# Edge rounds of a fused graph kernel: tile sums in two banks in turn, weights' sums made anew in each round, the third gather ahead of the edge rows, node products' parts made ahead of the rounds

## The reference, cut to what matters

```python
h = x @ W
agg = jnp.einsum('ben,bnf->bef', alpha, h)                      
beta = jax.nn.sigmoid((h @ a_gn)[:, None, :] + (agg @ a_ge)[:, :, None])
all_he = jax.nn.elu(beta[..., None] * h[:, None, :, :] + (1.0 - beta[..., None]) * agg[:, :, None, :])
logits2 = jnp.where(H[None, :, :] > 0, se[:, None, :], NEG)
coefs1 = jax.nn.softmax(logits2, axis=-1)
g = jnp.einsum('bne,benf->bnf', coefs1, all_he)
```

## Time and profile before

| | |
|---|---|
| median of 3 runs | 725.89 us (724.87 to 726.29) |
| the profiled execution's own time | 726.31 us |
| its span in the profile | 724.1 us |
| PE busy | 668.4 us, 92% of the span |
| DVE, ACT, POOL busy | 422.0, 340.6, 289.9 us |
| mean granted TensorE clock | 0.97 |
| the eight edge rounds | 102.8 to 195.8 us |

### The profile page before, as it was taken

One profiled execution on the slowest core, in us unless ns is written; L12 is line 12 of the kernel. 1 busy time (PEld: TensorE's weight loads), 2 busy tenths in 40 slices (PEclk: granted clock), 3 DMA queues, 4 the chain that ended last, 5 costly groups with the idle time before them and its releaser, 6 DMA issues.

```text
span 724.1 us, 9828 instructions
## 1 busy us (share of the span) xinstructions
PE 668.4 (92%) x3420; PEld 462.6 (64%) x3428; DVE 422.0 (58%) x966; ACT 340.6 (47%) x655; POOL 289.9 (40%) x267
## 2 busy tenths in 40 slices
PE   6898989788799989999999999999999999999993
PEld 2796766566566867633333348887777777778883
DVE  1675656767539852366878756314565767651166
ACT  0861234544366651265666643323446556455214
POOL 0270104565536720010324256122667676760045
PEclk9999999999989699999999999999999999999998
DMA  9120030000000027000100000000000000000013
GB/s 326 38 88 2 1 116 1 1 0 1 1 2 1 4 52 164 19 0 1 37 22 1 1 0 1 1 1 1 2 1 1 0 1 1 1 1 2 1 29 87
DMA packets 14995, 18.34 MB, mean 25 GB/s; under 512 B 10128, under 2 KB 10128, under 8 KB 14944
## 3 DMA queue, kind: packets, MB, share of 16 engines
q1 hardware_dynamic: 14432, 16.06, 7.7%
q10 hardware_dynamic: 512, 1.60, 0.6%
HBM read 11.37 MB, written 2.10 MB: 19 GB/s over the span
## 4 chain that ended last, share of the span: by engine, by line
PE 53%; POOL 8%; DVE 6%; ACT 4%; issue 2%; ACTq 0%; POOLq 0%; DVEq 0%
PE PS L1504 9%; PE PS L1391 7%; PE PS L1374 7%; PE PS L1517 5%; POOL LN_Y L163 4%; PE PS L1557 4%; PE PS L1546 4%; PE PS L182 2%; PE PS L1483 2%; PE PS L1490 2%; PE PS L189 2%; PE PS L1567 2%; DVE arena L2143 2%; DVE LN_ST L140 1%; PE PS L1420 1%
## 5 line engine op out<-in xcount | busy, mean ns | idle before, releaser
L2143 DVE SCALAR_TENSOR_TENSOR arena<-PS,WT,arena 128x256 f32<-128x256 f32 x160 | 77.5, 484 | 49.2 <-PE PS L1517 27.0
L1714 ACT ACTIVATE arena<-PS,spare 128x1024 f32<-128x1024 f32 x64 | 70.8, 1109 | 49.8 <-DVE spare L2080 49.6
L2080 DVE TENSOR_REDUCE spare<-PS 128x1 f32<-128x1024 f32 x64 | 75.6, 1219 | 23.8 <-PE PS L1374 23.7
L1504 PE MATMUL PS<-WH,KK 128*128 128x512 f32 x256 | 86.1, 402 | 0.1
L163 POOL TENSOR_TENSOR LN_Y<-LN_V,CN 128x16 f32<-128x16 f32 (+1 forms) x18 | 50.0, 2779 | 67.6 <-DVE LN_V L155 67.6
L1782 ACT ACTIVATE spare<-PS,WT 128x256 f32<-128x256 f32 x96 | 38.8, 471 | 63.7 <-DVE arena L2143 61.8
L1875 POOL TENSOR_TENSOR arena<-arena,spare 128x128 f32<-128x128 f32 x32 | 13.8, 433 | 134.2 <-DVE spare L2086 123.6
L1391 PE MATMUL PS<-arena 128*64 128x512 f32 x256 | 62.0, 605 | 1.5 <-POOL arena L1875 1.4
L1504 PEld LDWEIGHTS PS<-WH,KK 128*128 128x128 f32 x256 | 48.0, 187 | 16.7 <-issue 5.7
L1504 PE MATMUL PS<-WL,KK 128*128 128x512 f32 x128 | 50.0, 391 | 0.0
L1374 PE MATMUL PS<-arena 64*128 64x512 f32 x192 | 48.2, 617 | 1.4 <-ACT arena L1714 1.4
(11 more groups left out here) (293 smaller groups left out, 1496.8 us busy)
## 6 DMA issues: line engine op xcount, KB each, us to landing
arena<-in_adj_tr SPq DMA_DIRECT2D x8, 512.0 KB, 5.9
arena<-in_x_tr SPq DMA_DIRECT2D x4, 512.0 KB, 8.0
arena<-in_x_nat SPq DMA_DIRECT2D x1, 2048.0 KB, 9.0
arena<-arena SPq DMA_DIRECT2D x7, 256.0 KB, 2.8
arena<-arena SPq DMA_DIRECT2D x12, 128.0 KB, 2.3
spare<-in_w SPq DMA_DIRECT2D x2, 512.0 KB, 4.0
out<-arena SPq DMA_DIRECT2D x4, 256.0 KB, 3.1
out<-arena SPq DMA_DIRECT2D x8, 128.0 KB, 2.2
```

Of the source, the lines that this page charges most:

```text
L1504: ins = pe.matmul(acc, x[:, t % 2, b, :], w[:, k, c], start=(first and n == 0), stop=(not first and n == 2), skip_group_check=True)
L1714: act.activation(EF[2 * (i % RING) + par], banks("S", 2 * i + par).rearrange("p a c -> p (a c)"), ACT.Exp, bias=NMX[:, i, par:par + 1], ac ...
L2080: dve.tensor_reduce(NMX[:, i, par:par + 1], banks("S", 2 * i + par), AX.XY, ALU.max, negate=True).then_inc(max_ready, 1)
L2143: dve.scalar_tensor_tensor(acc, PS[:, four_banks(t, j), d * F:(d + 1) * F], WT[:, e:e + 1], acc, ALU.mult, ALU.add).then_inc(acc_step, 1)
```

## The change

- The sums of the tiles lie in bank 4 for even tiles and in bank 7 for odd ones, so PE zeroes a bank without waiting for the copy of the tile before (it waits for that of the tile before the last one).
- The weights' sums no longer run on over a tile: each round starts them afresh in bank 5, ACT copies them out to a new ZR (128 x 8) and POOL adds ZR into ZS, which it has zeroed at the start. POOL's addition waits for ACT's copy (`zr_out`) and stands at the end of the round, ahead of L383 and L387. PE waits for the copy of the round before (`zr_out`) ahead of the edge rows, as these write bank 5 too. DVE's reciprocal waits for the additions (`zs_added`).
- PE has gather C ahead of the edge rows. DVE has shift A ahead of the interval tests.
- All eight `high` stand on ACT behind the tanh (L484), ahead of the second industry copy; all eight `low` on POOL ahead of the register loads. PE waits for all of them ahead of the first gather.

```diff
@@ -289,7 +289,13 @@
 iota = CN[:, C_IOTA:C_IOTA + ROUND].rearrange("p (c n) -> p c n", n=P)
-SMALL_AT, ZN_AT = CHUNKS * E, 0
+SMALL_AT, ZN_AT = CHUNKS * E, 3 * P
+ZR = sb("ZR", [P, B])
+zr_out, zs_added = sem("zr_out"), sem("zs_added")
+
+def sums_bank(t):
+    return 4 + 3 * (t % 2)
+
 A_, B_, C_ = range(CHUNKS)
@@ -351,6 +357,7 @@
         pool.memset(zero16[:, :], 0.0).then_inc(zero_set, 1)
+        pool.memset(ZS[:, :, :], 0.0)
         pool.wait_ge(sl, 1)
@@ -362,8 +369,8 @@
-        low(0)
-        low(1)
+        for t in range(NT):
+            low(t)
         first = first_rounds(pool)
@@ -376,8 +383,8 @@
                                        ALU.mult).then_inc(w_ready, 1)
-            if t + 2 < NT:
-                low(t + 2)
+                pool.wait_ge(zr_out, j + 2)
+                pool.tensor_tensor(ZS[:, t, :], ZS[:, t, :], ZR[:, :], ALU.add).then_inc(zs_added, 1)
             if t >= 1:
@@ -483,14 +490,17 @@
                            bias=wt(W_FCB, 1)).then_inc(the_done, 1)
+
+        def high(t):
+            act.activation(HPH[:, t, :], HP[:, t, :], ACT.Copy).then_inc(hph_ready, 1)
+
+        for t in range(NT):
+            high(t)
         industry_out(1)
...
-        def high(t):
-            act.activation(HPH[:, t, :], HP[:, t, :], ACT.Copy).then_inc(hph_ready, 1)
-
         def edges_out(dst, done):
@@ -508,12 +518,11 @@
         act.activation(AGS[:, :], PS[:, 7, :], ACT.Copy).then_inc(agh_ready, 1)
-        high(0)
         first = first_rounds(act)
+        act.activation(ZR[:, :], zero16[:, 0:B], ACT.Copy).then_inc(zr_out, 1)
         industry_out(3)
...
         act.activation(AGM1[:, :], bits(AGS[:, :]), ACT.Copy, scale=-1.0).then_inc(agn_ready, 1)
-        high(1)
         industry_out(4)
@@ -553,11 +562,9 @@
                 likely()
-            if t + 2 < NT:
-                high(t + 2)
-            act.wait_ge(acc_done, first[t + 1] + 1)
-            act.activation(GN[:, t, :], PS[:, 4, :], ACT.Copy)
-            act.activation(ZS[:, t, :], PS[:, 7, ZN_AT:ZN_AT + B], ACT.Copy).then_inc(acc_out, 1)
+                act.wait_ge(acc_done, j + 2)
+                act.activation(ZR[:, :], PS[:, 5, ZN_AT:ZN_AT + B], ACT.Copy).then_inc(zr_out, 1)
+            act.activation(GN[:, t, :], PS[:, sums_bank(t), :], ACT.Copy).then_inc(acc_out, 1)
@@ -744,10 +751,10 @@
                 mix(A_, 2)
+                shift(A_, 2)
                 dve.wait_ge(selg_ready, j + 1)
...
                 from_first(at).then_inc(ns_half, 1)
-                shift(A_, 2)
                 dve.wait_ge(ns_half, j + 2)
@@ -765,9 +772,10 @@
             if t >= 1:
-                dve.wait_ge(acc_out, t)
+                dve.wait_ge(zs_added, first[t])
                 dve.reciprocal(ZS[:, t - 1, :], ZS[:, t - 1, :]).then_inc(rn_ready, 1)
         dve.wait_ge(acc_out, NT)
+        dve.wait_ge(zs_added, first[NT])
         dve.reciprocal(ZS[:, NT - 1, :], ZS[:, NT - 1, :]).then_inc(rn_ready, 1)
@@ -965,7 +973,7 @@
         pe.wait_ge(agn_ready, 1)
-        pe.wait_ge(hpl_ready, 1)
+        pe.wait_ge(hpl_ready, NT)
         pe.wait_ge(nsg_ready, 1)
@@ -975,22 +983,21 @@
         for t in range(NT):
-            if t >= 1:
-                pe.wait_ge(acc_out, t)
-            pe.matmul(PS[:, 4, :], zero16[:, 0:P], zero16[:, :], start=True, stop=False, skip_group_check=True)
-            pe.matmul(PS[:, 7, ZN_AT:ZN_AT + B], zero16[:, 0:P], zero16[:, 0:B], start=True, stop=False, skip_group_check=True)
-            pe.wait_ge(hpl_ready, min(t + 2, NT))
+            if t >= 2:
+                pe.wait_ge(acc_out, t - 1)
+            pe.matmul(PS[:, sums_bank(t), :], zero16[:, 0:P], zero16[:, :], start=True, stop=False, skip_group_check=True)
             with pe.Fori(first[t], first[t + 1]) as j:
...
                     pe.wait_ge(w_ready, CHUNKS * j + (c + 1))
-                    return pe.matmul(PS[:, 4, :], NST[:, c, :], S1[:, c, :], start=False, stop=True, skip_group_check=True)
-
+                    return pe.matmul(PS[:, sums_bank(t), :], NST[:, c, :], S1[:, c, :], start=False, stop=True, skip_group_check=True)
+
+                pe.wait_ge(z_ready, CHUNKS * j + 1)
+                gather(t, C_)
+                pe.wait_ge(zr_out, j + 1)
                 pe.wait_ge(ns_ready, j + 2)
                 edge_rows(t_next)
-                pe.wait_ge(z_ready, CHUNKS * j + 1)
-                gather(t, C_)
                 pe.wait_ge(nst_out, j + 1)
@@ -1007,8 +1014,8 @@
                 for c in range(CHUNKS):
-                    ins = pe.matmul(PS[:, 7, ZN_AT:ZN_AT + B], NST[:, c, :], CC[:, c, :], start=False, stop=True,
-                                    skip_group_check=True)
+                    ins = pe.matmul(PS[:, 5, ZN_AT:ZN_AT + B], NST[:, c, :], CC[:, c, :], start=(c == 0),
+                                    stop=(c == CHUNKS - 1), skip_group_check=True)
                 ins.then_inc(acc_done, 1)
```

## The result

The changed kernel took 761.96 us, the median of 4 runs (761.63 to 762.42); the kernel before took 726.05 on the same chip (724.87 to 726.29). The ratio is 1.050, 95% interval 1.048 to 1.052. The direction was forecast, the size was not: 732.1 us, with a range up to 736.8.

A forecast was written before the change was run, and what follows sets the result against it. Rounds were bound by the PE and DVE chain to the first scatter, with POOL's queue to take over. Terms 3.0 + 1.2 + 0 - 0.5 + 1.0 + 1.5 = + 6.2 gave 732.1 us; range over the cases 726.8 to 736.8.

The forecast's parts named there:

- sum of + 6.2 us: Whole kernel: 3.0 + 1.2 + 0 - 0.5 + 1.0 + 1.5 us slower, giving 732.1 us.
- rival C: Edge rounds: two opened waits bring two to three further low-clock stretches, 1.3 us each; 735 to 737 us, chance 0.16.
- The prediction's last sentence: Wrong if rounds 2 to 6 scatter before T + 4.3, or more or fewer half-clock rounds make over 3 us.
- 0 in itself: PE's gather C, moved from a covered place into the idle stretch behind T, costs nothing: 0 us.
- The wait for L623 came behind that one and ended later: 0: Two banks: PE's dropped wait for ACT's copy ahead of the zeroing was covered by a later wait: 0 us.
- POOL's queue paces rounds 2 to 7: POOL sets the first scatter at T + 4.9 (4.4 to 5.4): + 3.0 us, and + 1.2 in round 7; chance 0.61.
- Edge rows, turn, round 1: Edge rows about T + 1.5, unhindered scatter T + 3.8, turn done by T + 4; round 1 unchanged, about 10.6 us.
- Round 0: First round, POOL empty: earlier edge rows count, - 0.5 us (0 to - 1.2).
- Front: Ahead of the rounds: POOL's eight parts meet seven DVE instructions and delay L712's loop, + 1.0 us (0 to + 1.3).
- End: End of the stage: POOL still has the addition, L383 and L387 for tile 6, + 1.5 us (1.3 to 1.7).
- A: Rounds 2 to 6: POOL's steps fit before the first product is needed, DVE's relief decides; 724.2 us, chance 0.12.
- B: Whole kernel: gains and losses cancel, POOL's queue at its lower bound, one low-clock stretch less; 725.9 us, chance 0.11.

The follow-up runs named there:

- e3: The changed kernel with matmuls of zeros in both PE waits of a round, 5 behind the edge rows and 6 ahead of the first scatter: 736.78 us.
- e1: The changed kernel with POOL's addition of ZR behind the two output steps of the tile before: 740.11 us.
- e4: The changed kernel with gather C behind the edge rows again, POOL's queue left as changed: 752.3 us.
- e8: The changed kernel with POOL's addition behind the output steps and gather C behind the edge rows again: 726.28 us.
- e14: The changed kernel plus PE's old wait for ACT's copy of the tile just done, ahead of the zeroing: 745.38 us.
- e10: e1 plus PE's old wait for ACT's copy of the tile just done, ahead of the zeroing: 724.32 us.
- e2: The kernel before with POOL's two output steps of the previous tile waiting for the round's end: 729.26 us.
- e11: The changed kernel with only PE's wait behind the edge rows filled, by 5 matmuls of zeros: 739.07 us.
- e12: The changed kernel with only PE's wait ahead of the first scatter filled, by 6 matmuls of zeros: 742.74 us.
- e9: e1 plus 5 matmuls of zeros in PE's wait behind the edge rows: 721.66 us.
- e16: The kernel before plus 5 matmuls of zeros (384 columns) ahead of the edge rows' wait: 723.09 us.
- e15: e1 plus 8 matmuls of zeros once, ahead of round 0: 737.14 us.
- e17: e1 plus 13 matmuls of zeros once, ahead of round 0: 731.5 to 745.0 us, ratio 1.0126.

## Why the prediction was right in its sign and wrong in its size

**The term of the clock failed.** The sum of + 6.2 us has no term for the clock; about 25 of the 36 us are the clock. It stood in rival C alone, as "Two to three further stretches, 1.3 each". There the sign and the places were right: it named the two waits behind the edge rows and before the first scatter. The number was low, four more than before in rounds 2 to 7, and the price far too low. 1.3 was read from rounds in which the clock was down for 3.4 us (164.6 to 168.0). Now it stays down over most of the round (136.7 to 146.9). Before, the fall was followed at once by gather C; now by the wait for POOL, scatter A and the small sums. Whether that is the reason for its length is not shown. The round at 0.69 costs 16.78 - 12.37 = 4.4 us, with e3's round as the measure. From T of round 0 to T of round 7 the changed kernel took 109.43 us and e3 87.63, 21.8 less; with the 3.9 by which e3's round 0 ended earlier that is the 25. The prediction's last sentence names this as a sign of being wrong: rounds at half clock that make up more than 3 us.

**"0 in itself" for gather C** failed with it. Its time was hidden before and after, as said; what it did where it stood was not, since it was the one piece of wide work among edge rows, turn and wait. Moved, it leaves a stretch of 4 us with 1.17 us of matmuls in it. It cost 9.7 to 13.8 us (e1, e4, e8).

**"The wait for L623 came behind that one and ended later: 0"** for the two banks failed in the same way. As a wait the old one was indeed covered. But it cut PE's idle time in two, ahead of gather C and behind it, and put back it returned 16.6 us to the changed kernel and 15.8 to e1 (e14, e10).

**POOL's queue paces rounds 2 to 7:** right in four of the six, and under-sized. In one of the others DVE's comparison, itself held back beside POOL, came last, in the other it tied with the product; the turn stood at T + 4.76 and T + 4.51, not by T + 4. The first scatter came at T + 5.43 in five of the six rounds (4.94 in the other), not 4.9, at the upper end of 4.4 to 5.4. Of the sum, the addition took 0.60, L394 1.59 against 1.27, and the first of the two L384 about 1.36 (2.40 - 1.04) beside DVE's L749. All three are meetings with DVE; alone the addition took 0.20, at 231.33 below. By the Trainium skill ("SBUF — State Buffer", section "SBUF: two separate sides") a DVE instruction with two SBUF inputs and a GpSimd instruction exclude each other for a whole instruction. The trace agrees, with 5.43, and with the L749 that started 0.05 us behind an L394 of 1.26 and took 1.75 instead of 0.69. The term is 5 x 1.11 + 1.74 = 7.3 at most, instead of 4.2. On the kernel before, POOL's two steps kept behind the round's end cost 3.3 (e2).

**Edge rows, turn, round 1:** the relief of DVE was forecast at T + 1.5 for the edge rows and T + 3.8 for an unhindered scatter; measured T + 1.20, and T + 3.78 in e1. Round 1 took 10.62, as said. Rounds 2 to 7 at full clock (forecast 11.5 to 12.0) can be seen only where the clock holds: 12.0 in e14, 11.9 and 12.4 in e11, 12.4 in e3 and e12.

**Round 0:** forecast - 0.5, measured + 3.4. Its low stretch, from 106.6 to 110.0 before, is now from 109.4 to 119.6: the clock again.

**Front:** + 1.9 instead of + 1.0, and by another step than the one named. POOL's parts started at 64.32 and ended at 74.2, as worked out, and the chain behind the old L695 (now L702) lost only some 0.3. But the first part met a tiny DVE instruction at 64.34, on which PE waits. Of before, and behind it of the changed kernel:

```profile
64.64 0.23 DVE L688 TENSOR_SCALAR kst<-CN,PS 8x22 f32<-8x22 f32 x1
...
65.12 0.19 PE L910 MATMUL PS<-CN,kq 8*1 8x9 f32 x2 [1.95 <-DVE kq L689]
```

```profile
64.34 1.28 DVE L695 TENSOR_SCALAR kst<-CN,PS 8x22 f32<-8x22 f32 x1
...
65.87 0.19 PE L918 MATMUL PS<-CN,kq 8*1 8x9 f32 x2 [3.02 <-DVE kq L696]
```

PE's wait grew from 1.95 to 3.02 us, and from 68 to 72 us the granted clock was 0.50 to 0.54, where it had been 0.74 and 1.00. The sum left out who else runs on DVE when the moved parts begin.

**End:** forecast + 1.5, measured 1.74. POOL's last addition, product and sum, and the next stage, in the order worked out:

```profile
231.33 0.20 POOL L387 TENSOR_TENSOR ZS<-ZS,ZR 128x8 f32<-128x8 f32 x1 [5.12 <-ACT ZR L566]
231.78 1.04 POOL L390 TENSOR_TENSOR arena<-arena,ZS 128x512 f32<-128x512 f32 x1 [0.24 <-issue]
232.96 1.52 POOL L394 TENSOR_TENSOR arena<-arena 128x512 f32<-128x512 f32 x1
...
236.65 1.75 PE L1249 MATMUL PS<-CN,arena 128*128 128x128 f32 x7 [5.61 <-PEq L77]
```

**Rivals.** A would have needed a first L384 that ends before T + 3.7, and it ended at T + 4.88 at the earliest. e9 is what A was meant to be, the relief with its clock kept: 721.66. e8 took B's time with 726.28, but by other terms. C's own sum, 732.1 + 2.6 to 3.9, is 734.7 to 736.0 and not 735 to 737.

## What to carry to other kernels

Where PE waits in each turn of a loop, do not price a moved piece of work by its own time alone: look at what PE does on both sides of each wait, at the granted clock in windows of 2 us, and ask how the loop would look with that clock low for most of a turn. A wait that is covered by a later one may still matter by where it stands. Before a POOL instruction is made to wait for something late, count all that stands behind it, each beside DVE at its lengthened price. And when a kernel gets slower by more than its waits, fill them with matmuls of zeros: the run tells in one step about how much is the clock, and may be the better kernel.

## What the runs showed of the hardware that was not expected

- A wait more made the kernel 16 us faster, twice (761.96 to 745.38, 740.11 to 724.32).
- A wait of 1.35 us in each round, in an engine marked busy for 12.52 of 13.90 us, goes with a granted clock that falls to 0.50 in six of seven rounds (e1), and filled it goes with 1.00 in all seven (e9).
- Matmuls of zeros were enough to hold the clock: 25.2, 18.5 and 3.1 us by e3, e9 and e16.
- A short instruction can cost its engine over five times its time beside the other engine: DVE's 8x22 at 64.34 took 1.28 us against 0.23, POOL's 128x8 addition 0.60 against 0.20.
- How many rounds lose their clock differs between executions of e1, e15 and e17 (730.3 to 741.0 us, and 745.0 once) and hardly in the changed kernel (761.6 to 762.4). A rule that gives the rounds was not found.
- The clock stayed at 0.50 for 9 us while PE was marked busy without a gap (138 to 146 us in the changed kernel).
